# A gated cross-attention block: layer norm inside attention, hidden units on the partitions, int8 products

## The chip, the cores and the metric

The kernel runs on one core of a Trainium2 chip. The metric is the time of one execution on the device in microseconds (us). The engines are TensorE (PE; its weight loads are shown as PEld), VectorE (DVE), ScalarE (ACT), GpSimd (POOL) and SyncE (SP), which issues all DMAs here. Each engine works through its own list of instructions in order; semaphores tie the lists together.

## The reference

Four batches of 1024 tokens, width 512. A cross-attention with 8 heads of 64 over a context of 1024 keys is followed by a feed-forward part with ternary weights, 8-bit activations and a convolution over the tokens:

```python
x = x + tanh(g_x) * xattn(ctx, layernorm(x), mask, ...)      # 4 x 1024 x 512
x = x + tanh(g_f) * ffn(layernorm(x), w1, conv_w, conv_b, w2)

def act_quant(x):       # per token: the largest |x| becomes 127
    scale = 127.0 / clip(max(abs(x), axis=-1), 1e-05)
    return clip(round(x * scale), -128, 127) / scale
def bit_linear(x, w):  return einsum('bsd,hd->bsh', act_quant(x), weight_quant(w))

h = bit_linear(x, w1)                      # 512 -> 2048 hidden units
h = silu(depthwise_conv1d(h, conv_w, conv_b))   # 3 taps along the tokens, per unit
return bit_linear(h, w2)                   # 2048 -> 512
```

The second `act_quant` needs, for each token, the maximum over all 2048 hidden units before any of that token's values can be rounded.

## The kernel before

The program has three parts. First come the projections (up to about 670 us), which the change doesn't touch. Then comes attention, `c_pe`, `c_dve`, `c_act` and the POOL loop at L656 to L667 (to 1412 us), and last the feed-forward part, `ffn` on each engine.

**Attention.** A loop of 134 steps (`MACROS`, variable `s`), written out and the same on every engine, sets the order. 32 steps belong to one batch. A step has two units (`score`, `product`: 128 keys by 512 queries of a pair of heads) and two `tops`, which run 22 units ahead: they multiply keys and queries once more (L1244) into PSUM banks 4 and 5, and DVE takes the row minimum from them (L926) to give the softmax its shift. Each of the two banks holds one `tops`, so TensorE may write the next only when DVE has read the last (`dve_free4`, `dve_free5`). ACT takes the exponential of each unit (L684), POOL adds seven of each eight probability tiles to a sum (L667). Every fourth step the sums are turned into the scale of the result (L950 to L968). In the first eight steps of the next batch TensorE also does `project` (L1224 to L1226), eight token tiles of 128, whose result DVE adds to `bx` (`finish`, L975); SP stores `bx` to memory as x2.

**Feed-forward part.** Per batch: x2 comes back from memory as `xn`; DVE does the layer norm of the second half of the block there (`ln_steps`, L862 to L910), with 127/max per token; TensorE turns the rounded values (L1407). The steps for batch b+1 stand between those of batch b's last stage; those of batch 0 stand alone. Then come 16 tiles of 128 hidden units (the units on the partitions, 1024 tokens along the free axis): TensorE multiplies (`first`, L1419), DVE scales (`scaled`, L1158), ACT and POOL and DVE do the three taps (L800, L804, L672, L1179), TensorE turns the tile so that tokens lie on the partitions (L1448), ACT takes silu from PSUM (L823), DVE the maxima (L1163). When all 16 are through, the hidden values of 128 tokens at a time are rounded (L1168, L1170), shifted back to integers by ACT (L810, L815), turned again by TensorE (L1434), copied by ACT (L832, L840) and multiplied by w2 (L1461); DVE adds the result to x2 (L1207). The whole batch goes out in one DMA.

## Time and profile before

| | us |
|---|---|
| median of 3 runs (lowest to highest) | 1928.52 (1926.75 to 1930.60) |
| the profiled execution | 1929.86 |
| its span | 1928.0 |
| PE busy in the span | 1684.4 (87%) |
| DVE busy | 1216.9 (63%) |
| ACT busy | 780.3 (40%) |
| POOL busy | 729.0 (38%) |
| attention, last projected tile added | 1412.8 |
| first scaled tile of the feed-forward part | 1441.5 |

A part's busy share says which engine could bound it; the idle time ahead of an instruction, and the engine that ended it, say who waited for whom. The granted clock of TensorE has two levels here, 2.4 GHz (1.0 in the rows) and 1.2 GHz.

### The profile page before, as it was taken

To read this page: it belongs to the slowest core of one execution; us is meant where nothing else is said; L and a number is where in the kernel's file an instruction comes from. 1 tells how busy PE (TensorE), PEld (TensorE's weight loads), DVE (VectorE), ACT (ScalarE), POOL (GpSimd) and SP (SyncE) were. 2 spreads that over 40 slices of the span, in tenths; PEclk is the share of its full clock that TensorE was granted. 3 is DMA by queue.
4 is the path that set the end of the run, shared out by engine and by line. 5 is a ranking of instruction groups with operands and counts; after the bars stand their busy time and mean duration, and the time that the engine had idled before them with its cause. 6 is when DMAs were issued, how large, how long until landed. Compare 5 with 4: busy or idle time off the path is not lost.

```text
span 1928.0 us, 24398 instructions
## 1 busy us (share of the span) xinstructions
PE 1684.4 (87%) x8738; PEld 1038.8 (54%) x8738; DVE 1216.9 (63%) x2270; ACT 780.3 (40%) x793; POOL 729.0 (38%) x317
## 2 busy tenths in 40 slices
PE   6887899999997699999999999999856785967867
PEld 5666678888885344455445444544433443534434
DVE  6777645343433567755765676465269979799793
ACT  2111122222210044433442344245318766787676
POOL 1121000000000088866885688578606134062340
PEclk9989999999998599999999999999979798997988
DMA  6656547444444511114111412041130030120201
GB/s 233 229 181 206 179 170 243 154 149 152 171 145 152 180 56 56 56 66 143 56 57 66 143 57 100 12 143 35 44 131 1 1 131 0 38 92 0 88 1 44
DMA packets 104676, 200.59 MB, mean 104 GB/s; under 512 B 7568, under 2 KB 27024, under 8 KB 104592
## 3 DMA queue, kind: packets, MB, share of 16 engines
q1 hardware_dynamic: 104592, 199.49, 29.5%
q8 instruction: 50, 0.82, 0.2%
q14 instruction: 34, 0.28, 0.0%
HBM read 127.90 MB, written 71.57 MB: 103 GB/s over the span
## 4 chain that ended last, share of the span: by engine, by line
PE 62%; issue 19%; POOL 7%; DVE 6%; DMA 5%; SPq 1%; ACT 1%; POOLq 0%; DVEq 0%; ACTq 0%
PE ps L1260 13%; PE ps L1272 12%; PE ps L1224 9%; PE ps L1226 9%; PE ps L1225 9%; PE ps L1244 6%; DMA wraw<-in_w2T 5%; POOL h_first L672 4%; POOL h_third L672 2%; PE ps L1285 2%; DVE junk L926 1%; PE ps L1461 1%; DVE h_first L1179 1%; POOL acc L667 1%; DVE gp L1158 1%
## 5 line engine op out<-in xcount | busy, mean ns | idle before, releaser
L667 POOL TENSOR_TENSOR acc<-acc,pr 128x1024 f32<-128x1024 f32 x192 | 457.7, 2384 | 118.7 <-ACT pr L684 99.6
L684 ACT ACTIVATE pr<-ps,mcol 128x1024 f32<-128x1024 f32 x256 | 284.3, 1114 | 405.1 <-PE ps L1260 402.3
L926 DVE CUSTOM_DVE_ANT_0 junk<-ps,mbias 128x512 bf16<-128x512 f32 x512 | 333.4, 689 | 171.8 <-PE ps L1244 168.0
L1272 PE MATMUL ps<-pr,vv 128*64 128x512 f32 x1024 | 273.3, 616 | 0.0
L672 POOL TENSOR_TENSOR h_first<-h_first,last_tap 128x1024 f32<-128x1024 f32 x44 | 104.8, 2385 | 306.2 <-ACT last_tap L804 306.2
L650 POOL MEMSET nmt<- 128x128 f32 x1 | 0.2, 204 | 449.1 <-DMA w_ternary<-wtb 449.1
L1244 PE MATMUL ps<-kh,qh 64*128 64x512 f32 x512 | 136.8, 475 | 26.3 <-DVE nmv L926 17.6
L1244 PEld LDWEIGHTS ps<-kh,qh 64*128 64x128 f32 x512 | 57.5, 193 | 148.3 <-issue 101.7
L1419 PE MATMUL ps<-xiT,w1q 128*128 128x512 bf16 x512 | 125.1, 393 | 5.9 <-ACT xiT L790 5.9
L1461 PE MATMUL ps<-w2q,hq 128*128 128x512 bf16 x512 | 120.8, 390 | 2.5 <-ACT hq L840 1.8
L667 POOL TENSOR_TENSOR acc<-pr 128x1024 f32<-128x1024 f32 x32 | 76.8, 2399 | 110.8 <-ACT pr L684 110.8
L1260 PE MATMUL ps<-qh,kh 64*128 64x512 f32 x512 | 116.2, 445 | 0.0
L1448 PE MATMUL ps<-ident,h_first 128*128 128x128 f32 x352 | 57.8, 317 | 66.2 <-DVE h_first L1179 51.8
L1260 PE MATMUL ps<-qh,kl 64*128 64x512 f32 x512 | 102.5, 392 | 0.0
L1260 PE MATMUL ps<-maug,aug 64*128 64x512 f32 x512 | 102.3, 391 | 0.0
L1260 PE MATMUL ps<-ql,kh 64*128 64x512 f32 x512 | 102.0, 390 | 0.0
L1224 PE MATMUL ps<-chh,wsh 128*128 128x512 f32 x256 | 99.7, 389 | 1.7 <-DVE chl L1091 1.7
L1224 PE MATMUL ps<-wsh,chh 128*128 128x512 f32 x256 | 99.7, 389 | 0.3 <-DVE cst L1133 0.3
L1226 PE MATMUL ps<-wsh,chl 128*128 128x512 f32 x256 | 99.6, 389 | 0.0
L1225 PE MATMUL ps<-wsl,chh 128*128 128x512 f32 x256 | 99.6, 389 | 0.0
L1225 PE MATMUL ps<-chl,wsh 128*128 128x512 f32 x256 | 99.6, 389 | 0.0
L1226 PE MATMUL ps<-chh,wsl 128*128 128x512 f32 x256 | 99.6, 389 | 0.0
(152 smaller groups left out, 3179.7 us busy)
## 6 DMA issues: line engine op xcount, KB each, us to landing
craw<-in_ctxT SPq DMA_DIRECT2D x8, 2048.0 KB, 9.7
xa<-in_x SPq DMA_DIRECT2D x8, 1024.0 KB, 6.4
wraw<-in_w1T SPq DMA_DIRECT2D x16, 512.0 KB, 7.3
...
q_split<-kqh SPq DMA_DIRECT2D x32, 256.0 KB, 2.0
q_split<-kql SPq DMA_DIRECT2D x32, 256.0 KB, 2.3
...
k_split<-kqh SPq DMA_DIRECT2D x32, 256.0 KB, 2.2
```

The costliest lines, as they stand in the source:

```text
L667: nc.gpsimd.tensor_tensor(acc[:, blk % 2, :], first, pr[:, (8 * blk + j) % NP, :], ALU.add).then_inc(pool_acc, 1)
L672: nc.gpsimd.tensor_tensor(h[j % 3], h[j % 3], last_tap[j % 2][:], ALU.add).then_inc(pool_tap, 1)
L684: act.activation(pr[:, u % NP, :], ps[:, 2 * (u % 2):2 * (u % 2) + 2, :].rearrange("p a t -> p (a t)"), ACT.Exp, bias=mcol[:, (u // 64) * ...
L926: dve.tensor_tensor_reduce(out=junk[:, e, :], in0=ps[:, 4 + e, :], in1=mbias[:, b % 2, kk * CH:(kk + 1) * CH], scale=-1.0, scalar=3.0e38, ...
L1224: pe.matmul(acc, lh, rh, start=k == 0, stop=False)
L1225: pe.matmul(acc, lh, rl, start=False, stop=False)
L1226: last = pe.matmul(acc, ll, rh, start=False, stop=k == n - 1)
L1244: last = pe.matmul(ps[:, 4 + e, :], qh[g % 3][64 * e:64 * e + 64, i * P:(i + 1) * P], kh[g % 3][64 * e:64 * e + 64, kk * CH:(kk + 1) * CH] ...
L1260: last = pe.matmul(ps[:, 2 * (u % 2) + e, :], of_keys[64 * e:64 * e + 64, :], of_tokens[64 * e:64 * e + 64, :], start=w == 0, stop=w == 3)
L1272: last = pe.matmul(ps[64 * e:64 * e + 64, 6 + blk % 2, :], vv[:, g % 2, j, 64 * e:64 * e + 64], pr[:, u % NP, e * CH:(e + 1) * CH], start= ...
L1419: last = pe.matmul(ps[:, 2 * (j % 2) + t, :], w1q[:, k, j * P:(j + 1) * P], xiT[:, k, t * 512:(t + 1) * 512], start=k == 0, stop=k == KD - 1)
L1461: last = pe.matmul(ps[:, i % 2, :], hq[:, i % 2, j, :], w2q[:, j, :], start=j == 0, stop=j == KH - 1)
```

## The change

The layer norm of batches 0 to 2 moves into attention, in the steps of the following batch; it works in `bx` itself, so x2 isn't read back for it. The turned integers go to memory (`xt_d`) and come back as `xiT`, already turned. For the last batch the same work stands between the hidden tiles of batch 0.

Beside that the second half of the feed-forward part is built anew. The hidden values stay with the units on the partitions (`hh`). TensorE turns each tile once, in float32, only so that DVE can take the maxima over the units (`highest`). The scale of each token is then spread over all partitions by TensorE (`spread`, into banks 6 and 7); DVE multiplies each unit tile by it and writes int8 (`quantised`), ACT widens int8 to bfloat16 (`widen`), and the product takes the tile as it lies. Six token tiles are multiplied in the stage itself, the two that find no free PSUM banks are left for the opening of the next batch (`left_over`). The scaling happens in PSUM in place, the taps read PSUM, and the output goes out in 32 DMAs of 128 tokens.

```diff
+        STATS, NORMS, ROUNDS, XT = {}, {}, {}, {}
+        for b in range(B - 1):
+            m0 = 32 * (b + 1)
+            MOMENTS[m0 + NT], RSTD[m0 + NT + 2], SCALES[m0 + NT + 11] = b, b, b
+            for i in range(NT):
+                STATS[m0 + i] = b, i
+                NORMS[m0 + NT + 3 + i] = b, i
+                ROUNDS[m0 + NT + 12 + i] = b, i
+                XT[m0 + NT + 13 + i] = b, i
+        MP = [6, 0, 6, 0, 6, 0] + [(2, 6, 0)[j % 3] for j in range(KH - 6)]
+        EARLIER = {j: max(i for i in range(j) if MP[i] == MP[j]) for j in range(KH) if MP[j] in MP[:j]}
+        PLACE = [0, 1, 2, 3, 4, 5, 2, 3]
...
@@ SP, in attention
                 if g % PAIRS == 1 and b:
                     store_x2(b - 1)
-                    sp.wait_ge(sp_x2_out, 16 * b)
-                    sp.dma_start(bx[:], base_d[b * S:(b + 1) * S, :].rearrange("(j p) d -> p j d", p=P)).then_inc(sp_bx, 16)
+                if g % PAIRS == 3 and b:
+                    store_xt(b - 1)
+                    load_bx(b)
                 if g + 1 < NG:
                     max_rows(g + 1)
...
@@ ACT, in attention
             for s in range(MACROS):
+                if s - 1 in XT:
+                    turned(*XT[s - 1])
                 for a in range(2):
                     if 2 * s + a < UNITS:
                         exp(2 * s + a)
                     if a == 0 and s - 2 in ZBLK:
                         upper(ZBLK[s - 2])
+                if s - 1 in MOMENTS:
+                    deviation(act, MOMENTS[s - 1])
+                if s in ROUNDS:
+                    integers(act, *ROUNDS[s])
...
@@ DVE, at the end of a step of attention
+                if s in NORMS:
+                    normalise(dve, *NORMS[s])
+                    tallest(dve, *NORMS[s])
+                if s in ROUNDS:
+                    rounded(dve, *ROUNDS[s])
...
+        def normalise(dve, b, i):
+            dve.wait_ge(dve_rs, b + 1)
+            dve.wait_ge(sp_x2_out, 16 * (b + 1))
+            dve.tensor_scalar(bx[:, i, :], bx[:, i, :], mv2[:, i, 0:1], rs2[:, 1, i:i + 1], ALU.subtract, ALU.mult).then_inc(dve_nm, 1)
+        def rounded(dve, b, i):
+            dve.wait_ge(dve_sc, 4 * (b + 1))
+            dve.tensor_scalar(bx[:, i, :], bx[:, i, :], asc[:, i:i + 1], MAGIC, ALU.mult, ALU.add).then_inc(dve_xr, 1)
+        def integers(act, b, i):
+            act.wait_ge(dve_xr, NT * b + i + 1)
+            act.activation(bxi[:, i, 0:D], bx[:, i, :], ACT.Copy, bias=-MAGIC).then_inc(act_xi, 1)
+            def turned(b, i):
+                act.wait_ge(pe_xt, NT * b + i + 1)
+                act.activation(bxi[:, i, D:2 * D], ps[:, 5, :].bitcast(BF16)[:, 0:D], ACT.Copy).then_inc(act_xt, 1)
...
@@ TensorE, in attention: ahead of the first tops of a step, and at a step's end
+                if n >= LEAD and (n - LEAD) % 2 == 0 and (n - LEAD) // 2 - 1 in XT:
+                    b, i = XT[(n - LEAD) // 2 - 1]
+                    pe.wait_ge(act_xt, NT * b + i + 1)
...
+                if s in XT:
+                    b, i = XT[s]
+                    pe.wait_ge(dve_free5, use5["b", min(2 * s + LEAD, UNITS - 2) + 1] + 1)
+                    if b or i:
+                        pe.wait_ge(act_xt, NT * b + i)
+                    turn_xi(pe, b, i, 5, 0)
...
@@ TensorE, feed-forward part
+                unit_tile(b, 1)
+                for j in range(KH):
+                    if b and j < 4:
+                        left_over(b - 1, 6 + j // 2, j % 2)
+                    if j + 2 < KH:
+                        unit_tile(b, j + 2)
+                    if j >= 2:
+                        turn_h(b, j - 2)
+                turn_h(b, KH - 2)
+                turn_h(b, KH - 1)
+                pe.wait_ge(dve_hm, 5 * b + 4)
+                spread(hsc, 6).then_inc(pe_inv, 1)
+                if b + 1 < B:
+                    spread(adq[:, b + 1, :], 0).then_inc(pe_row, 1)
...
+                for j in range(KH):
+                    pe.wait_ge(act_hq, KH * b + j + 1)
+                    if j == KH - 1 and b + 1 < B:
+                        unit_tile(b + 1, 0)
+                    product(b, j, range(6))
...
@@ DVE, feed-forward part
+                scaled(b, 0)
+                if b:
+                    for i in range(4):
+                        finish(b - 1, i)
+                scaled(b, 1)
+                if b:
+                    finish(b - 1, 4)
+                    finish(b - 1, 5)
+                for j in range(KH):
+                    if b and j in (2, 4):
+                        finish(b - 1, 5 + j // 2)
+                    first_tap(b, j)
+                    if j == KH - 1:
+                        third_tap(b, j)
                     if j >= 3:
+                        highest(b, j - 3)
+                    if j + 2 < KH:
+                        scaled(b, j + 2)
...
+                for j in range(KH - 3, KH):
+                    highest(b, j)
+                unit_scales(b)
+                for j in range(KH):
+                    quantised(b, j)
```

How the lists move, at three places. First ACT in attention, in the part of a batch where the norm is rounded and turned. Before (L684 is the exponential, L692 the copy of a scaled result):

```order
L692 ACTIVATE uh<-un 128x512
L684 ACTIVATE pr<-ps,mcol 128x1024 x8
L692 ACTIVATE uh<-un 128x512
L684 ACTIVATE pr<-ps,mcol 128x1024 x8
L692 ACTIVATE uh<-un 128x512
```

Now (L703 is the exponential; L694 is `integers`, L715 `turned`, L711 the copy of a scaled result):

```order
L703 ACTIVATE pr<-ps,mcol 128x1024 x2
L694 ACTIVATE bx<-bx 128x512
L715 ACTIVATE bx<-ps 128x512
L703 ACTIVATE pr<-ps,mcol 128x1024 x2
L694 ACTIVATE bx<-bx 128x512
L715 ACTIVATE bx<-ps 128x512
L703 ACTIVATE pr<-ps,mcol 128x1024
L711 ACTIVATE uh<-un 128x512
```

Between the two exponentials of one step and the two of the next there are now the copy that follows DVE's rounding and, behind it, the copy out of bank 5.

Second, DVE in attention, one step in which a block's sums are finished. Before (L926 is the row minimum and its readout, L954 to L963 the scale):

```order
L926 ISA nmv 128x1
L954 RECIPROCAL zr<-zt 128x16
L956 STREAM_TRANSPOSE rb<-zr 128x512
L926 ISA junk,nmv<-ps,mbias 128x512
L926 ISA nmv 128x1
L926 ISA junk,nmv<-ps,mbias 128x512
L926 ISA nmv 128x1
L963 TENSOR_TENSOR un<-ps,rb 128x512
L926 ISA junk,nmv<-ps,mbias 128x512
```

Now (L878 is `normalise`, L882 `tallest`, L908 the row minimum, L945 the former L963):

```order
L936 RECIPROCAL zr<-zt 128x16
L938 STREAM_TRANSPOSE rb<-zr 128x512
L908 ISA junk,nmv<-ps,mbias 128x512
L908 ISA nmv 128x1
L908 ISA junk,nmv<-ps,mbias 128x512
L908 ISA nmv 128x1
L945 TENSOR_TENSOR un<-ps,rb 128x512
L878 TENSOR_SCALAR bx<-bx,mv_118,rs_119 128x512
L882 TENSOR_REDUCE amax<-bx 128x1
L908 ISA junk,nmv<-ps,mbias 128x512
```

Two instructions stand between the last row minimum of one step and the first of the next; in the later steps of the batch it is one, L895 (`rounded`).

Third, DVE at the end of a batch's 16 tiles in the feed-forward part. Before:

```order
L1179 SCALAR_TENSOR_TENSOR h_first<-gp,convw,h_first 128x1024
L1163 TENSOR_REDUCE hmax<-hT 128x8 x3
L1186 TENSOR_REDUCE hm<-hmax 128x8
L1188 TENSOR_SCALAR hm<-hm 128x8
L1190 RECIPROCAL hsc<-hm 128x8
L1192 TENSOR_SCALAR hsc<-hsc 128x8
L1193 TENSOR_SCALAR hdq<-hm,cst 128x8
L1168 TENSOR_SCALAR hT<-hT,hsc 128x1024 x2
L1170 TENSOR_SCALAR hT<-hT,hsc 128x2048 x3
```

Now (L1149 is `scaled`, L1153 `first_tap`, L1163 `highest`, L1182 `quantised`, L1190 `finish`):

```order
L1153 SCALAR_TENSOR_TENSOR hh<-ps,convw,hh 128x1023
L1158 SCALAR_TENSOR_TENSOR hh<-ps,convw,hh 128x1023
L1163 TENSOR_REDUCE hmax<-ps 128x8 x4
L1167 TENSOR_REDUCE hm<-hmax 128x8
L1169 TENSOR_SCALAR hm<-hm 128x8
L1171 RECIPROCAL hsc<-hm 128x8
L1173 TENSOR_SCALAR hsc<-hsc 128x8
L1174 TENSOR_SCALAR hdq<-hm,cst 128x8
L1182 TENSOR_TENSOR q_126<-hh,ps 128x1024 x16
L1149 TENSOR_TENSOR ps<-ps,row 128x1024
L1190 SCALAR_TENSOR_TENSOR x2t<-ps,hdq,x2t 128x512 x4
L1149 TENSOR_TENSOR ps<-ps,row 128x1024
```

The maxima at the end each follow a turned tile in the one pair of banks 4 and 5, and the finished outputs of the batch stand among the first tiles of the next. In the new code `unit_tile(b, j)` waits for `first_tap` of tile `EARLIER[j]`, the last to hold its banks, and `turn_h(b, j)` for `highest(b, j - 1)`.

## Rows read from the trace of the kernel before

**Rows 1.** Busy time in stretches: span, then PE, PEld, DVE, ACT, POOL; clock, DMA

```profile
750.00:1340.00 590.00, 585.58 (x3287) 284.93 (x3285) 370.85 (x1004) 240.72 (x234) 427.94 (x181) 1.00 0.22 79
1563.00:1637.00 74.00, 48.44 (x248) 28.57 (x246) 68.36 (x50) 53.71 (x49) 38.69 (x16) 0.88 0.20 72
```

**Rows 2.** Timeline of one step of attention: start, duration, engine, line, [idle before]

```profile
916.48 0.49 PE L1244 MATMUL ps<-kh,qh 64*128 64x512 f32 x2
917.15 2.38 POOL L667 TENSOR_TENSOR acc<-pr 128x1024 f32<-128x1024 f32 x1 [1.34 <-ACT pr L684]
918.24 0.08 DVE L926 DVE_READ_ACCUMULATOR2_ANT nmv<- 128x1 f32 x1
918.95 0.39 PE L1244 MATMUL ps<-kh,qh 64*128 64x512 f32 x2
919.49 0.69 DVE L926 CUSTOM_DVE_ANT_0 junk<-ps,mbias 128x512 bf16<-128x512 f32 x1 [0.89 <-PE ps L1244]
```

**Rows 3.** Timeline: POOL adds and DVE instructions that overlap them

```profile
771.71 2.39 POOL L667 TENSOR_TENSOR acc<-pr 128x1024 f32<-128x1024 f32 x1 [1.33 <-ACT pr L684]
773.07 1.58 DVE L937 TENSOR_SCALAR mbias<-mbias 128x1024 f32<-128x1024 f32 x1
...
811.89 2.39 POOL L667 TENSOR_TENSOR acc<-pr 128x1024 f32<-128x1024 f32 x1 [1.34 <-ACT pr L684]
831.96 2.39 POOL L667 TENSOR_TENSOR acc<-pr 128x1024 f32<-128x1024 f32 x1 [1.31 <-ACT pr L684]
...
1606.49 2.36 POOL L672 TENSOR_TENSOR h_first<-h_first,last_tap 128x1024 f32<-128x1024 f32 x1 [2.20 <-ACT last_tap L804]
1607.56 2.38 DVE L1179 SCALAR_TENSOR_TENSOR h_first<-gp,convw,h_first 128x1024 f32<-128x1024 f32 x1
```

**Rows 4.** Groups of instructions after 1400 us: count, busy us, mean ns

```profile
L886 DVE TENSOR_SCALAR xn<-xn,mv,rs 128x512 f32<-128x512 f32 x32 | 15.0, 544 | 0.1
L891 DVE TENSOR_REDUCE amax<-xn 128x1 f32<-128x512 f32 x32 | 19.6, 683 | 0.0
L908 DVE TENSOR_SCALAR xn<-xn,asc 128x512 f32<-128x512 f32 x32 | 15.4, 480 | 0.0
L810 ACT ACTIVATE hi<-hT 128x1024 bf16<-128x1024 f32 x8 | 8.0, 1049 | 13.1 <-DVE hT L1168 13.1
```

**Rows 5.** Timeline between attention and the feed-forward part, and its third batch's start

```profile
1412.08 0.75 DVE L975 SCALAR_TENSOR_TENSOR bx<-ps,cst,bx 128x512 f32<-128x512 f32 x1 [3.17 <-PE ps L1226]
1441.49 1.23 DVE L1158 TENSOR_TENSOR gp<-ps,row 128x1024 f32<-128x1024 f32 x1 [5.32 <-PE ps L1419]
...
1684.71 1.23 DVE L1158 TENSOR_TENSOR gp<-ps,row 128x1024 f32<-128x1024 f32 x1 [3.63 <-PE ps L1419]
```

**Rows 6.** Timeline of a hidden tile in the second batch, and DVE two tiles on

```profile
1602.88 1.21 DVE L1158 TENSOR_TENSOR gp<-ps,row 128x1024 f32<-128x1024 f32 x1
1604.01 1.36 DVE L1179 SCALAR_TENSOR_TENSOR h_third<-gp,convw,h_third 128x1024 f32<-128x1024 f32 x1
1604.12 1.24 ACT L800 ACTIVATE h_first<-gp,convb,convw 128x1024 f32<-128x1024 f32 x1
1605.50 1.09 PE L1448 MATMUL ps<-ident,h_third 128*128 128x128 f32 x8 [0.73 <-DVE h_third L1179]
...
1610.98 1.21 DVE L1158 TENSOR_TENSOR gp<-ps,row 128x1024 f32<-128x1024 f32 x1
```

**Rows 7.** Timeline: eight turns at the lower clock, and sixteen products at the higher

```profile
1632.13 1.97 PE L1448 MATMUL ps<-ident,h_first 128*128 128x128 f32 x8 [0.35 <-DVE h_first L1179]
...
1676.68 3.62 PE L1461 MATMUL ps<-w2q,hq 128*128 128x512 bf16 x16
```

**Rows 8.** DMA issues: count, KB each, median us from issue to landing

```profile
v_full<-vst SPq DMA_DIRECT2D x32, 256.0 KB, 2.0
bx<-base SPq DMA_DIRECT2D x4, 2048.0 KB, 8.7
row_max<-mt SPq DMA_DIRECT2D x16, 16.0 KB, 1.4
```

More of the change, by code:

```diff
@@ L21 @@
 BF16 = mybir.dt.bfloat16
+INT8 = mybir.dt.int8
 ALU = mybir.AluOpType
@@ L269, in flamingo_gated_block @@
         dve_free5 = sem("dve_free5")
[L270 removed]
+        dve_top = sem("dve_top")
         dve_inv = sem("dve_inv")
@@ new lines, in taps @@
+            def taps(b, j):
+                act.wait_ge(dve_g, KH * b + j + 1)
+                act.activation(hh[:, j, :], flat(MP[j]), ACT.Identity, bias=convb[:, j:j + 1], scale=convw[:, j, 1:2]).then_inc(act_tap, 1)
+                if j == KH - 1:
+                    return
+                n = (KH - 1) * b + j
+                if n >= 2:
+                    act.wait_ge(pool_tap, n - 1 if j >= 2 else (KH - 1) * b)
+                act.activation(tap[:, j % 2, 0:S - 1], flat(MP[j])[:, 1:S], ACT.Copy, scale=convw[:, j, 2:3]).then_inc(act_tap, 1)
@@ new lines, in _ @@
+            scale_row(0)
+            for b in range(B):
+                for j in range(KH):
+                    taps(b, j)
+                    if j >= 2:
+                        silu(b, j - 2)
+                    if b == 0 and j == 1:
+                        deviation(act, LAST_B)
+                    if b == 0 and j >= NT:
+                        integers(act, LAST_B, j - NT)
+                silu(b, KH - 2)
+                silu(b, KH - 1)
+                if b + 1 < B:
+                    scale_row(b + 1)
+                if b == 0:
+                    for u in range(NT // 2):
+                        turned_last(u)
+                for j in range(KH):
+                    widen(b, j)
@@ L1210, in _, with scaled @@
-            for step in ln_steps(dve, 0):
-                step()
-            for s in range(3):
-                dve.memset(gp[:, s, 0:1], 0.0)
-                dve.memset(gp[:, s, S + 1:S + 2], 0.0)
-            with dve.Fori(0, B - 1) as b:
-                ffn(b, True)
-            ffn(B - 1, False)
+            def scaled(b, j):
+                dve.wait_ge(pe_h, KH * b + j + 1)
+                if j == 0:
+                    dve.wait_ge(act_row, b + 1)
+                dve.tensor_tensor(flat(MP[j]), flat(MP[j]), row[:, b % 2, :], ALU.mult).then_inc(dve_g, 1)
@@ L1220, in split_mm @@
+            for i in range(NT):
+                finish(LAST_B, i)
         def split_mm(pe, acc, lhs, rhs, n):
@@ L1227, in split_mm, with turn_xi @@
             return last
-        def ln_row(pe, b):
-            pe.wait_ge(dve_ln, b * LN_DVE_N + LN_DVE["diag"])
-            for t in range(2):
-                last = pe.matmul(ps[:, 2 + t, :], ones[:], diag[:, 4 * t:4 * t + 4, :], start=True, stop=True)
-            last.then_inc(pe_row, 1)
+        def turn_xi(pe, b, i, bank, part):
+            pe.wait_ge(act_xi, NT * b + i + 1)
+            for k in range(KD):
+                last = pe.transpose(ps[:, bank, :].bitcast(BF16)[:, (part * KD + k) * P:(part * KD + k + 1) * P], bxi[:, i, k * P:(k + 1) * P], identb[:])
+            last.then_inc(pe_xt, 1)
         def c_pe(pe):
@@ L1470, in _, with spread @@
-            ln_row(pe, 0)
-            for u in range(NT // 2):
-                ln_turn(0, u)
-            pe.wait_ge(sp_ffw, 32)
-            with pe.Fori(0, B - 1) as b:
-                ffn(b, True)
-            ffn(B - 1, False)
+            def spread(cols, bank):
+                for i in range(NT):
+                    last = pe.matmul(ps[:, bank + i // 4, i % 4 * P:(i % 4 + 1) * P], cols[:, i:i + 1].broadcast_to([P, P]), ident[:],
+                                     start=True, stop=True)
+                return last
@@ L1479 @@
+            for i in (6, 7):
+                for part in range(2):
+                    left_over(LAST_B, i, part)
 _INS = ["x", "ctxT", "mask", "mask_cols", "g_x", "g_f", "wsT", "bk_cols", "b_v", "wtT", "bq_cols", "woT", "b_out",
```

564 lines of the change are left out of this document (247 added, 317 removed).

## The prediction

> **What bounds the kernel now.** I read the busy time in stretches first. From 750 to 1340 us TensorE is busy 585.6 of 590 us at the full clock, DVE 370.9, POOL 427.9 [rows 1]. So attention is bound by TensorE, and whatever makes TensorE wait there lengthens the kernel. In the hidden tiles of the feed-forward part DVE is busy 68.4 of 74 us and TensorE 48.4 [rows 1]; DVE sets the pace there. Then I read timelines. Two first scalings two batches apart, 1441.49 and 1684.71, give 121.6 us a batch [rows 5]. Between the last `finish` of attention (1412.08 + 0.75) and the first scaling lie 28.7 us in which the layer norm of batch 0 runs alone [rows 5]. Two things can be won, then: that gap, and part of the 486.5 us from 1441.5 to the end of the span. The price falls in attention.
>
> **Part 1, the gap.** After the change TensorE spreads the scales at once (8 small matmuls, estimate 1.6 us), ACT copies the row (1024 columns, like the 1.05 us of [rows 4]), and DVE scales: first scaling 3.5 us after `finish`, not 28.7. That is -25.2 us.
>
> **Part 2, the hidden tiles.** Before, two tiles take 8.10 us (1602.88 to 1610.98), 4.05 each [rows 6]. DVE's instructions follow each other closer than their lengths: 1.13 us after a 1.21 (1602.88 to 1604.01) [rows 6]. Now DVE does `scaled`, `first_tap` and `highest`, 1.13 + 1.20 + 1.13 = 3.46 us. The second length is that of the unblocked tap, 1.36 at most [rows 6]; the longer one of 2.38 overlaps a POOL add [rows 3], and the new tap reads PSUM. That in-place writing to PSUM costs no more than writing to SBUF no row shows; I take the 1.21 and give 4.05 a tile as the upper end. TensorE needs 8 x 0.22 for the matmuls (16 in 3.62 [rows 7]) and 1.09 for the turns [rows 6], 2.9 us: hidden. ACT has two taps and a silu, each below the 1.24 of [rows 6], some 3.3 us: just hidden.
>
> Not all tiles run at 3.46. Tiles 0 to 5 use two pairs of banks, so DVE waits in a circle: tap 1.2, matmuls of tile j+2 2.1 (1.75 plus the drain), scaling 1.2: 4.5 us. In a batch after the first:
> opening, two scalings, six outputs of 0.67 (0.75 long [rows 5]) and one wait for the banks, 7.0; five tiles at 4.5, 22.5; nine at 3.46, 31.1; last two taps, third tap and two maxima, 6.0; three turns that alternate with their maxima in one pair of banks, 3 x 2.4, and 2.2 more since TensorE drops to the lower clock when it idles there (eight turns 1.97 against 1.09 [rows 6, 7]), 9.4; the scale arithmetic 1.3; `spread` 2.9 at the lower clock (estimate, 8 loads and matmuls). Sum 80.2.
> Then `quantised` makes a tile in 1.13, ACT widens it in 1.05 [rows 4], TensorE multiplies six token tiles in 6 x 0.22 = 1.3 us. TensorE bounds this stage, and it starts late: the second `spread`, the row copy and the first widening come first, 4.8; 15 products, two of them at half clock, 22; the next batch's first tile, 2. In all 109.0 us, against 121.6.
> Batch 0 has no outputs of an earlier batch among its tiles but the last batch's norm: 8 x (0.54 + 0.68 + 0.48) [rows 4] and some waits for POOL, net 18, and four more copies of ACT ahead of the first widening, 4: 131. The last batch ends with 32 products left over (6.9), the outputs and one DMA of 256 KB (2.0 [rows 8]): 118. Sum 131 + 109 + 109 + 118 = 467 against 486.5: -19.5 us. Bounds: -35 if the clock stays up in the last turns and first products, 0 if the nine tiles stay at 4.05.
>
> **Part 3, the norm in attention.** TensorE begins a `tops` at 916.48, DVE has read both banks at 918.32, the next begins at 918.95, and DVE starts on it at 919.49 after 0.89 idle [rows 2]. Work put into that gap costs TensorE what exceeds about 0.9 + 0.6 = 1.5 us; the 0.6 is 918.95 less 918.32, the time by which a bank is free too early. `normalise` and `tallest` are 0.54 + 0.68 = 1.22 [rows 4]: nothing, if nobody is in their way. But POOL is. A DVE `tensor_scalar` that began at 773.07 ended at 774.65, 0.55 after the POOL add that ran to 774.10, and took 1.58; the tap at 1607.56 ended 1.09 after POOL's 1608.85 [rows 3]. Both did their work after POOL's instruction, not beside it. POOL's seven adds of 2.39 fill 16.7 of the 20.07 us of four steps (811.89 to 831.96 [rows 3]), 83%. So `normalise` waits up to 2.39, on average half of it: 1.2 + 0.3 + 0.68 = 2.2, 0.7 over the gap, 24 times: +17 us (bounds 0 and 24 x 1.9 = 45).
>
> The Trainium skill ("SBUF — State Buffer", section "SBUF: two separate sides") says the port pair that DVE and GpSimd share is an exclusive lock for a whole instruction, against DVE instructions in a 2-port mode or with two SBUF inputs. The rows above agree, and the rule speaks against this change: both moved `tensor_scalar` are of that kind, while `quantised`, `scaled` and `highest` are not. Were it a sharing of bandwidth instead, a `normalise` would grow by tenths of a us, stay in the gap, and the sum would be that of the first rival.
>
> The rounding is dearer, since three engines hang on it. In the steps of XT, counted from the second `tops`: DVE free at 1.84; `rounded` waits for POOL, done at 3.6 (1.4 + 0.3); ACT, whose list has `integers` ahead of `turned` ahead of the next exponential, does `integers` by 4.3 and `turned`, out of bank 5, by 5.0 (512 columns, 0.6 each, from 1.05 for 1024 [rows 4]). TensorE may not start the next `tops` before that; it would be there at 2.47 [rows 2] + 0.27 for four turns. It stands 2.4 us, 2.7 with the turns. Seven steps in each of batches 0 and 1; batch 2's fall where no `tops` are left (they run 22 units ahead of 256) and cost 0.3, as do the last steps. 14 x 2.7 + 10 x 0.3 = +41 us. Bounds: 14 x 1.3 + 3 = 21 if POOL is never in the way, 14 x 4.1 + 3 = 60 if always by a whole add.
>
> DMAs: SP now loads `bx` (2 MB, 8.7 us [rows 8]) only some 2.3 steps before the next group's scores, with `row_max` (1.4 [rows 8]) and its way back queued behind: 8.7 + 1.4 + 2.5 against 11.5 us, about 1.3 late, twice: +3. `x2` is stored in time for `normalise`. The statistics stand in the steps of `project`, where DVE idles 3 us before each `finish` [rows 5]: 0. The small scale arithmetic: +1. Attention: 17 + 41 + 3 + 1 = +62.
>
> **Sum.** 1929.9 (the profiled execution, span 1928.0 and 1.9 around it; 1.3 above the median) - 25.2 - 19.5 + 62 = 1947; as a median 1946.
>
> **Rivals.**
> Faster: the adds of POOL don't meet the moved instructions. As steps stretch, POOL idles more, and it already has 1.34 us idle ahead of a block's first add [rows 2]. Then `normalise` costs 0 and the XT steps 21, attention +22: 1928.5 - 44.7 + 22 = 1906. It decides at an attention cost of 45 us; below that the change wins. Against it: 83% of POOL's time is taken, and ACT's order alone gives the 21.
> Slower still: the hidden tiles gain nothing (writing into PSUM dear, or ACT's 3.3 us late): 9 x 0.59 x 4 = 21 more, 1967.
> The clock: with turns and matmuls at the lower clock a tile needs 1.97 + 3.5 = 5.5 us of TensorE, 2.0 more than 3.46, 64 times: +130, 2076. Against it: TensorE kept the higher clock at 2.9 of 4.05 us [rows 6], and 2.9 of 3.46 is more.
>
> **How the numbers follow.** The forecast 0.55 (own range 1924 to 1972), the first rival 0.33, the second 0.08, the clock 0.04. Slower by over 0.2% (the 3.9 us that a measurement can tell from no change): most of the forecast, 0.46, the last two, 0.12, a little of the first rival, 0.03: 0.61. Within: 0.06 + 0.02 = 0.08. Faster: 0.03 + 0.28 = 0.31. The range takes most of the first rival and the second: 1899 to 1977.
>
> **What would show it.** Right: ACT's `turned` ends about 5 us after the second `tops` of its step, and TensorE idles 2 to 3 us before the next; `normalise` and `rounded` in attention last on average well over 1 us; first scaling within 4 us of the last `finish`; a batch of the feed-forward part takes about 109 us with tiles of 4.5 and then 3.46. Wrong: these two at 0.5 us each in attention, attention longer by under 45 us, or a batch period away from 100 to 118.

## The result and the profile after

The changed kernel takes 1973.2 us (median of four runs, 1971.9 to 1978.0) where the kernel before took 1929.6 on the same chip: ratio 1.0233, interval 1.0212 to 1.0254. I had forecast 1946 with a range of 1899 to 1977. The direction and the range held; the loss is 43.6 us where I had 17.

The two profiled executions differ by 42.9 us of span (1970.9 less 1928.0). Four landmarks divide them: POOL's first addition of attention, the last `finish` (L957), the first scaling of the feed-forward part (L1149) and the end. Here are the rows of after, from the timelines of POOL and DVE (start, duration, engine, line, idle before and what ended it):

```profile
673.74 2.39 POOL L680 TENSOR_TENSOR acc<-pr 128x1024 f32<-128x1024 f32 x1 [55.57 <-ACT pr L703]
...
1485.14 0.75 DVE L957 SCALAR_TENSOR_TENSOR bx<-ps,cst,bx 128x512 f32<-128x512 f32 x1 [2.42 <-PE ps L1243]
1489.83 1.23 DVE L1149 TENSOR_TENSOR ps<-ps,row 128x1024 f32<-128x1024 f32 x1 [3.20 <-PE ps L1450]
...
1616.61 1.23 DVE L1149 TENSOR_TENSOR ps<-ps,row 128x1024 f32<-128x1024 f32 x1 [10.76 <-PE ps L1450]
1730.32 1.23 DVE L1149 TENSOR_TENSOR ps<-ps,row 128x1024 f32<-128x1024 f32 x1 [9.49 <-PE ps L1450]
1842.59 1.23 DVE L1149 TENSOR_TENSOR ps<-ps,row 128x1024 f32<-128x1024 f32 x1 [7.07 <-PE ps L1450]
```

| stage | before | after | difference | forecast |
|---|---|---|---|---|
| attention, POOL's first addition to last `finish` | 737.9 | 811.4 | +73.5 | +62 |
| last `finish` to first scaling | 29.4 | 4.7 | -24.7 | -25.2 |
| feed-forward part, first scaling to end | 486.5 | 481.1 | -5.4 | -19.5 |

(The rest, -0.5, lies before attention.) The gap is as forecast. Attention costs 11.5 more, the feed-forward part gives 14 less.

In attention TensorE is no longer the engine that is always busy. The busy time of the stretch of [rows 1], now:

```profile
750.00:1340.00 590.00, 554.45 (x2985) 264.42 (x2981) 398.67 (x1003) 236.09 (x245) 376.25 (x160) 0.98 0.22 76
```

TensorE stands still for 35.6 us of it, before for 4.4. What it waits for shows in the waits of that attention (engine, line, what it waited for: us in total, times, longest). ACT's copy that makes integers (L694) waits for DVE's rounding (L895), and TensorE's product for the row minima (L1263) for ACT's copy of the turned tile (L715):

```profile
ACT bx L694 <- DVE bx L895: 78.6, 21, 5.2
PE ps L1263 <- ACT bx L715: 21.5, 13, 2.5
```

Two such steps that follow each other in the timeline of after; POOL is in the way in the first and not in the second:

```profile
969.74 4.87 POOL L680 TENSOR_TENSOR acc<-acc,pr 128x1024 f32<-128x1024 f32 x2 [4.19 <-ACT pr L703]
972.85 2.05 DVE L895 TENSOR_SCALAR bx<-bx,asc 128x512 f32<-128x512 f32 x1
976.09 0.50 PE L1263 MATMUL ps<-kh,qh 64*128 64x512 f32 x2 [2.45 <-ACT bx L715]
...
982.93 0.40 PE L1249 MATMUL ps<-identb,bx 128*128 128x128 bf16 x4
...
983.68 0.45 DVE L895 TENSOR_SCALAR bx<-bx,asc 128x512 f32<-128x512 f32 x1
984.16 0.63 ACT L694 ACTIVATE bx<-bx 128x512 bf16<-128x512 f32 x1 [5.21 <-DVE bx L895]
984.70 0.58 ACT L715 ACTIVATE bx<-ps 128x512 bf16<-128x512 bf16 x1
985.33 0.50 PE L1263 MATMUL ps<-kh,qh 64*128 64x512 f32 x2 [0.87 <-ACT bx L715]
...
986.36 4.88 POOL L680 TENSOR_TENSOR acc<-acc,pr 128x1024 f32<-128x1024 f32 x2 [4.38 <-ACT pr L703]
```

In the first, POOL's two additions run to 974.6, the rounding takes 2.05 us where it takes 0.45 in the second, and TensorE stands still for 2.45 us where it does for 0.87. The second shows what ACT's order does by itself. TensorE has turned the tile by 983.3. Its copy (L715) needs nothing else, but ACT's list has L694 ahead of it, and that waits for a rounding of another tile; the copy, the exponential and the next product for the minima come that much later: 984.70 for the copy instead of 983.3. ACT had idled 5.2 us before.

How much each kind of step costs is read from POOL's first addition in every block of four steps. In after:

```profile
916.67 2.35 POOL L680 TENSOR_TENSOR acc<-pr 128x1024 f32<-128x1024 f32 x1 [1.34 <-ACT pr L703]
...
963.19 2.37 POOL L680 TENSOR_TENSOR acc<-pr 128x1024 f32<-128x1024 f32 x1 [1.42 <-ACT pr L703]
...
1026.95 2.36 POOL L680 TENSOR_TENSOR acc<-pr 128x1024 f32<-128x1024 f32 x1 [4.49 <-ACT pr L703]
1048.98 2.39 POOL L680 TENSOR_TENSOR acc<-pr 128x1024 f32<-128x1024 f32 x1 [1.33 <-ACT pr L703]
```

The same blocks in `no_norm` below, which has no layer norm in attention and whose attention is within 1.5 us of before's:

```profile
915.17 2.39 POOL L680 TENSOR_TENSOR acc<-pr 128x1024 f32<-128x1024 f32 x1 [1.33 <-ACT pr L703]
...
955.06 2.39 POOL L680 TENSOR_TENSOR acc<-pr 128x1024 f32<-128x1024 f32 x1 [1.35 <-ACT pr L703]
...
995.25 2.39 POOL L680 TENSOR_TENSOR acc<-pr 128x1024 f32<-128x1024 f32 x1 [1.33 <-ACT pr L703]
1015.37 2.39 POOL L680 TENSOR_TENSOR acc<-pr 128x1024 f32<-128x1024 f32 x1 [1.35 <-ACT pr L703]
```

A block stands between the shown ones in the first two distances. The two blocks with a `normalise` (steps 11 to 18 of the batch) take 46.52 against 39.89, +6.6 for eight steps. The two with the turnings take 63.76 against 40.19, +23.6, and the next, which holds the last copy, 22.03 against 20.12, +1.9. Over all three batches, against before: normalise +19.8, turnings of batches 0 and 1 +48.4, the last blocks (batch 2's rounding and turning) +5.3; sum 73.5.

In the blocks with a `normalise` an instruction that the change didn't touch grew too: L950 (`lower`), once a block, whose two inputs and output are in SBUF. The same one in after and in no_norm (where its line is L952):

```profile
940.82 2.29 DVE L950 TENSOR_TENSOR ul<-un,uh 128x512 fp32r<-128x512 f32 x1
```

```profile
934.16 0.69 DVE L952 TENSOR_TENSOR ul<-un,uh 128x512 fp32r<-128x512 f32 x1
```

POOL's addition runs from 940.21 to 942.56 in after; in no_norm the next one starts only at 935.22. Three times in this batch, in these two blocks and right behind them, L950 now falls beside an addition (917.47, 940.82, 963.37: 2.10, 2.29, 2.73 us); in no_norm and small_pool the same three take 0.69. DVE is busy 42.4 of the 46.5 us of the two blocks (its waits for POOL counted in), in no_norm 27.4 of 39.9.

In the feed-forward part the hidden tiles run at exactly the forecast pace. DVE in the third batch, where [rows 6] had 8.10 for two tiles:

```profile
1764.51 1.22 DVE L1149 TENSOR_TENSOR ps<-ps,row 128x1024 f32<-128x1024 f32 x1
...
1767.96 1.22 DVE L1149 TENSOR_TENSOR ps<-ps,row 128x1024 f32<-128x1024 f32 x1
```

3.45 us a tile. The loss is elsewhere: at the openings, where the outputs of the batch before (L1190) are finished, and at the end, where those of the last batch are. DVE after 1616.61, and the PE work behind it:

```profile
1617.75 2.72 DVE L1190 SCALAR_TENSOR_TENSOR x2t<-ps,hdq,x2t 128x512 f32<-128x512 f32 x4
...
1623.62 0.75 DVE L1190 SCALAR_TENSOR_TENSOR x2t<-ps,hdq,x2t 128x512 f32<-128x512 f32 x1 [1.24 <-DMA x2t<-x]
1625.72 0.75 DVE L1190 SCALAR_TENSOR_TENSOR x2t<-ps,hdq,x2t 128x512 f32<-128x512 f32 x1 [1.35 <-DMA x2t<-x]
1626.38 1.27 DVE L1153 SCALAR_TENSOR_TENSOR hh<-ps,convw,hh 128x1023 f32<-128x1023 f32 x1
...
1627.71 3.60 PE L1450 MATMUL ps<-xiT,w1q 128*128 128x512 bf16 x8 [4.88 <-DVE hh L1153]
```

The first tap starts 9.8 us after the scaling, and 11.0 in the two later openings, forecast 7.0. x2 has four tiles in SBUF; the load of tile k+3 waits until the store of tile k-1 is through, and with loads and stores in turn each takes 3.5 us to land (after's DMA table: `x2t<-x` and `out<-x2t`, 256 KB each), where I had taken 2.0 from [rows 8]. TensorE, idle for 4.9 us, restarts at the lower clock: 3.60 for eight matmuls that take 1.90 at 1619.20. At the end the last four outputs start 2.2 to 2.6 us apart (1960.28, 1962.83, 1965.08, 1967.55), each behind its load. In all DVE waits for these loads 20.6 us in 13 waits.

### The profile page after: what moved, and what is told of

Read it like the earlier page. It is cut to its first block and busy times, and to the rows that moved or that the text cites. A ratio compares the mean times of both kernels' runs of the same rounds, so it can differ in the third digit from the quotient of the medians.

```text
span 1970.9 us, 22933 instructions
## 1 busy us (share of the span) xinstructions
PE 1701.0 (86%) x8338; PEld 1028.1 (52%) x8338; DVE 1233.3 (63%) x2260; ACT 732.1 (37%) x825; POOL 715.3 (36%) x313
## 5 line engine op out<-in xcount | busy, mean ns | idle before, releaser
L908 DVE CUSTOM_DVE_ANT_0 junk<-ps,mbias 128x512 bf16<-128x512 f32 x512 | 332.3, 686 | 154.5 <-PE ps L1263 151.5
L703 ACT ACTIVATE pr<-ps,mcol 128x1024 f32<-128x1024 f32 x256 | 283.8, 1115 | 361.6 <-PE ps L1279 352.9
L1291 PE MATMUL ps<-pr,vv 128*64 128x512 f32 x1024 | 280.0, 630 | 0.0
L686 POOL TENSOR_TENSOR hh<-hh,tap 128x1023 f32<-128x1023 f32 x60 | 141.5, 2358 | 316.6 <-DVE hh L1153 259.2
L1263 PE MATMUL ps<-kh,qh 64*128 64x512 f32 x512 | 152.6, 489 | 57.0 <-DVE nmv L908 24.8
L1263 PEld LDWEIGHTS ps<-kh,qh 64*128 64x128 f32 x512 | 63.3, 194 | 199.6 <-issue 88.3
L1461 PE MATMUL ps<-ident,hh 128*128 128x128 f32 x512 | 81.5, 311 | 65.9 <-DVE hmax L1163 65.9
L1450 PE MATMUL ps<-xiT,w1q 128*128 128x512 bf16 x384 | 100.3, 409 | 29.3 <-DVE hh L1153 24.4
L1149 DVE TENSOR_TENSOR ps<-ps,row 128x1024 f32<-128x1024 f32 x64 | 78.4, 1225 | 67.9 <-PE ps L1450 67.9
L820 ACT ACTIVATE hh<-ps,convb,convw 128x1024 f32<-128x1024 f32 x64 | 77.1, 1205 | 102.8 <-DVE ps L1149 102.8
L1461 PEld LDWEIGHTS ps<-ident,hh 128*128 128x128 f32 x512 | 66.5, 161 | 91.7 <-issue 69.6
```

Source lines behind the costliest of these rows:

```text
L686: nc.gpsimd.tensor_tensor(hh[:, j, 0:S - 1], hh[:, j, 0:S - 1], tap[:, j % 2, 0:S - 1], ALU.add).then_inc(pool_tap, 1)
L703: act.activation(pr[:, u % NP, :], ps[:, 2 * (u % 2):2 * (u % 2) + 2, :].rearrange("p a t -> p (a t)"), ACT.Exp, bias=mcol[:, (u // 64) * ...
L908: dve.tensor_tensor_reduce(out=junk[:, e, :], in0=ps[:, 4 + e, :], in1=mbias[:, b % 2, kk * CH:(kk + 1) * CH], scale=-1.0, scalar=3.0e38, ...
L1149: dve.tensor_tensor(flat(MP[j]), flat(MP[j]), row[:, b % 2, :], ALU.mult).then_inc(dve_g, 1)
L1263: last = pe.matmul(ps[:, 4 + e, :], qh[g % 3][64 * e:64 * e + 64, i * P:(i + 1) * P], kh[g % 3][64 * e:64 * e + 64, kk * CH:(kk + 1) * CH] ...
L1291: last = pe.matmul(ps[64 * e:64 * e + 64, 6 + blk % 2, :], vv[:, g % 2, j, 64 * e:64 * e + 64], pr[:, u % NP, e * CH:(e + 1) * CH], start= ...
```

## The experiments

Ratios are to the kernel before on the same chip; "against after" is the difference of the two ratios (after 1.0233) times 1929.6. The kernels ran on four chips, so it is the ratios that are compared. The block columns are what the blocks of normalise steps and of turnings (batches 0 and 1) take more than before, in one profiled execution each. That of act_order took 1931.0 us, 7.7 less than its median: 42.0 less than after's, 33.6 of it in attention.

| kernel | us | ratio, interval | against after | normalise | turnings |
|---|---|---|---|---|---|
| after | 1973.2 | 1.0233, 1.0212 to 1.0254 | | +19.8 | +48.4 |
| no_norm | 1894.1 | 0.9840, 0.9815 to 0.9864 | -75.8 | -0.1 | 0.0 |
| act_order | 1938.7 | 1.0074, 1.0056 to 1.0091 | -30.7 | +19.9 | +17.4 |
| small_pool | 1922.1 | 0.9983, 0.9971 to 0.9995 | -48.2 | +1.6 | +23.7 |
| order_pool | 1905.3 | 0.9891, 0.9855 to 0.9927 | -66.0 | +1.5 | +8.1 |
| order_split | 1955.6 | 1.0144, 1.0089 to 1.0200 | -17.2 | +31.3 | +26.5 |
| on_act | 1908.9 | 0.9888, 0.9840 to 0.9936 | -66.6 | +3.5 | +8.6 |
| x2_eight | 1954.5 | 1.0151, 1.0131 to 1.0172 | -15.8 | +19.8 | +48.4 |
| on_act_x2 | 1896.0 | 0.9823, 0.9778 to 0.9868 | -79.1 | +3.3 | +8.7 |
| on_act_x2_again | 1896.0 | 0.9820, 0.9804 to 0.9836 | -79.7 | +3.2 | +8.8 |
| best | 1917.0 | 0.9947, 0.9934 to 0.9960 | -55.2 | +3.4 | +28.3 |

**no_norm: attention without the layer norm.** The loop is the one that fills STATS, NORMS, ROUNDS and XT; what sets the semaphores of the missing work is not shown.

```
-        for b in range(B - 1):
+        for b in range(0):
-                    sp.wait_ge(act_xt, NT * b + i + 1)
+                    sp.wait_ge(sp_x2_out, 16 * (b + 1))
-                                 bxi[:, i, D:2 * D].rearrange("p (k t) -> p k t", k=KD)).then_inc(sp_xt_out, 16)
+                                 w1q[:, :, i * P:(i + 1) * P]).then_inc(sp_xt_out, 16)
```

> Leaves out the whole layer norm of batches 0 to 2 inside attention (statistics, normalise, maxima, rounding, integers, turning, and the copies of the turned tiles); what it stores as the turned tiles is other data of the same size, at the end of the batch's output, and the feed-forward part runs as in the changed kernel (the turned integers of the last batch are made in the tail as before, with the others' scales set to 1). All of the lengthening of attention is the layer norm's: the last finish of attention falls from 1485.1 to 1412 or 1415 us, the time to about 1900. A rival: the DMA queue's new loads and stores cost a part that stays, 5 to 10 us, and the time is 1905 to 1910.

-75.8 us. Attention takes 739.3 us from POOL's first addition to the last `finish`, 1.5 more than before, with the loads and stores of the change still there (the turned tiles' store sends other data of the same size). So the layer norm is practically all of attention's lengthening, and the moved DMAs are at most 1.5 of it; the rival of 5 to 10 falls.

**act_order: the copy of the turned tile no longer behind the rounding.**

```
                     if a == 0 and s - 2 in ZBLK:
                         upper(ZBLK[s - 2])
+                    if a == 0 and s - 1 in ROUNDS:
+                        integers(act, *ROUNDS[s - 1])
...
-                if s in ROUNDS:
-                    integers(act, *ROUNDS[s])
```

> Same computation as the changed kernel. Only ScalarE's order differs in the attention of batches 1 and 2: the copy that makes the integers of a tile (L694) stands behind the first exponential of the next step instead of at the step's end, so the copy of the turned tile (L715), which the row maxima's next product waits for, no longer stands behind VectorE's rounding. Theory A (the order on ScalarE makes the round trip long: rounding, integers, turned copy, product of the maxima): the sixteen steps with a turning fall from 2.9 us extra each to about 1, the time falls by about 28 us, to 1945. Rival B (the rounding is late because GpSimd's addition holds VectorE off, and everything behind it is late whatever ScalarE's order is): less than 6 us, 1967 to 1973. What the profile is to show under A: ScalarE's wait for bx of VectorE (82.5 us in 22 waits) falls below 30 us.

-30.7, theory A. The turnings fall from +48.4 to +17.4, 1.1 us a step, the normalise blocks don't move. ACT's wait for the rounding is 3.0 us in two waits between 954 and 1020 us, 30.0 in seven in after; over the whole of attention it is 3.9, in after 78.6. The instructions are the same; only ACT's list differs. From the timeline of this kernel:

```profile
993.38 0.40 PE L1249 MATMUL ps<-identb,bx 128*128 128x128 bf16 x4
...
993.71 2.56 DVE L895 TENSOR_SCALAR bx<-bx,asc 128x512 f32<-128x512 f32 x1
993.82 0.60 ACT L715 ACTIVATE bx<-ps 128x512 bf16<-128x512 bf16 x1 [1.29 <-PE ps L1249]
...
994.75 0.40 PE L1263 MATMUL ps<-kh,qh 64*128 64x512 f32 x2
...
996.30 0.63 ACT L694 ACTIVATE bx<-bx 128x512 bf16<-128x512 f32 x1 [0.23 <-DVE bx L895]
```

Here a rounding of 2.56 us, held back by POOL (two additions, 991.09 to 995.99), runs beside the copy and TensorE's next product: TensorE doesn't see it.

**small_pool: POOL's additions cut to a sixteenth of their columns.** One takes 0.32 us instead of 2.38.

```
-  nc.gpsimd.tensor_tensor(acc[:, blk % 2, :], first, pr[:, (8 * blk + j) % NP, :], ALU.add)
+  nc.gpsimd.tensor_tensor(acc[:, blk % 2, 0:64], first[:, 0:64], pr[:, (8 * blk + j) % NP, 0:64], ALU.add)
```

> GpSimd adds only the first 64 of 1024 columns of each exponential (the rest of the softmax's sums is left out), so its additions hold VectorE off for a tenth of the time. Attention is otherwise the changed kernel's. Theory A (the layer norm's instructions cost mainly by the order of work and by their own length in VectorE's row, GpSimd's hold adds a part): the steps with a normalise fall from 0.83 to near 0.2 us extra, those with a rounding from 2.9 to about 2, in all -30 to -40 us, about 1938. Rival B (GpSimd's hold on VectorE is nearly all of it): -60 us or more, 1910. Rival C (the hold costs nothing beside TensorE): within 5 us of 1973.

-48.2, between A and B, and A's share for each kind of step was too small. The normalise steps lose all but 1.6 of 19.8 us; the turnings halve. The groups of DVE's instructions on `bx` between 900 and 1450 us (count, busy us, mean ns, idle before), first in act_order:

```profile
L895 DVE TENSOR_SCALAR bx<-bx,asc 128x512 f32<-128x512 f32 x24 | 33.2, 1388 | 0.0
L878 DVE TENSOR_SCALAR bx<-bx,mv,rs 128x512 f32<-128x512 f32 x24 | 25.2, 1052 | 0.0
...
L882 DVE TENSOR_REDUCE amax<-bx 128x1 f32<-128x512 f32 x24 | 16.5, 686 | 0.8
```

and in small_pool (its lines are one higher):

```profile
L883 DVE TENSOR_REDUCE amax<-bx 128x1 f32<-128x512 f32 x24 | 16.5, 686 | 0.8
L879 DVE TENSOR_SCALAR bx<-bx,mv,rs 128x512 f32<-128x512 f32 x24 | 12.8, 531 | 0.0
L896 DVE TENSOR_SCALAR bx<-bx,asc 128x512 f32<-128x512 f32 x24 | 11.2, 470 | 0.0
```

The `tensor_scalar` falls from 1052 to 531 and from 1388 to 470 ns; even one of eight columns (`amax`, three times), from 1269 to 161. The reduction on the same tile is the same to the ns. The Trainium skill ("SBUF — State Buffer", section "SBUF: two separate sides", under "Who interferes with whom") says just this: `tensor_scalar` can take the port pair that DVE shares with GpSimd, a `tensor_reduce` on trn2 never does. The rows agree.

**order_pool: both together.** act_order's and small_pool's edits.

> act_order with GpSimd adding only 64 of 1024 columns (the rest of the softmax's sums is left out). The question is whether the two causes, ScalarE's order and GpSimd's hold on VectorE, are together all of the turning steps' price. Additive theory: act_order left 0.8 to 1.8 us per turning step, small_pool left 1.4; together 0 to 0.3 each, attention is within 4 us of that of the kernel without a layer norm (no_norm, 1894.1), 1895 to 1900. Rival (a third cause: the product for the row maxima that waits for the turned tile's copy): 0.6 us or more per turning step stays, 1905 or more.

1905.3: the additive theory fails, attention is 10.2 us longer than no_norm's and not 4. The rival's time is met by a little, its cause isn't: the turnings keep 8.1 us, 0.5 a step, but between 954 and 1020 us no product waits for the turned tile's copy. ACT's order took 31.0 of the 48.4, POOL's hold 24.7, both 40.3 and not 55.7: they overlap. My reading, argued from the lists, is that a rounding that POOL holds back costs most where the copy stands behind it. With act_order POOL's hold is still worth 9.3 (17.4 less 8.1). What stays is mostly the turning's own time on TensorE. Two steps' first score products in order_pool, with the turning (L1250) between them, then the same two in no_norm:

```profile
972.72 0.51 PE L1280 MATMUL ps<-qh,kh 64*128 64x512 f32 x2
...
977.45 0.40 PE L1250 MATMUL ps<-identb,bx 128*128 128x128 bf16 x4
977.77 0.50 PE L1280 MATMUL ps<-qh,kh 64*128 64x512 f32 x2
```

```profile
971.51 0.50 PE L1284 MATMUL ps<-qh,kh 64*128 64x512 f32 x2
...
976.22 0.50 PE L1284 MATMUL ps<-qh,kh 64*128 64x512 f32 x2
```

The step takes 5.05 us with the turning and 4.71 without, and TensorE doesn't stand still ahead of L1250. Sixteen times 0.34 are 5.4 of the 8.1 us. In the waits between 954 and 1020 us the turning's weight load stands against DVE's minimum for 4.1 us, but that load overlaps other products and its wait costs nothing here.

**order_split: normalise in the middle of the step.** Besides act_order's edit:

```
                     if n < UNITS:
                         tops(n)
+                    if a == 0 and s in NORMS:
+                        normalise(dve, *NORMS[s])
...
-                    normalise(dve, *NORMS[s])
                     tallest(dve, *NORMS[s])
```

> Same computation as the changed kernel. ScalarE's order as in act_order (1938.7 us), and on VectorE the normalise stands behind the step's first pair of row maxima, its maximum still at the step's end, so that each single instruction falls into a gap of VectorE's row. Theory A (what the 24 normalise steps cost, 0.83 us each, is two instructions in one gap of VectorE's row that is too short for both): they fall to 0.3, -13 us, 1926. Rival B (each of the two instructions waits for GpSimd's addition to end, wherever it stands: in small_pool the same steps cost 0.1): no gain, 1936 to 1941, or a loss.

Against theory A, and rival B's "or a loss": 13.5 us slower than act_order. I had argued with the room that a gap leaves; what counts is when POOL begins. DVE and POOL of this kernel:

```profile
927.11 2.38 DVE L878 TENSOR_SCALAR bx<-bx,mv,rs 128x512 f32<-128x512 f32 x1
```

```profile
926.84 4.86 POOL L680 TENSOR_TENSOR acc<-acc,pr 128x1024 f32<-128x1024 f32 x2 [1.46 <-ACT pr L703]
```

In its new place `normalise` comes 0.3 us after the addition that the same step's exponential has released, and waits out nearly all of it; its mean goes from 1052 to 1464 ns. The turnings rose as well, from 17.4 to 26.5 us, and no run says by what.

**on_act: the two `tensor_scalar` on ACT.** Besides act_order's edit, for batches 0 to 2 (the semaphores, DVE's small product for `nb2` and the lines taken from DVE's list are not shown):

```
+        def normed(act, b, i):
+            act.activation(bx[:, i, :], bx[:, i, :], ACT.Identity, bias=nb2[:, i:i + 1], scale=rs2[:, 1, i:i + 1])
+        def whole(act, b, i):
+            act.activation(bx[:, i, :], bx[:, i, :], ACT.Copy, bias=MAGIC, scale=asc[:, i:i + 1])
...
+                    if a == 0 and s in NORMS:
+                        normed(act, *NORMS[s])
                     if a == 0 and s - 1 in ROUNDS:
                         integers(act, *ROUNDS[s - 1])
+                    if a == 0 and s in ROUNDS:
+                        whole(act, *ROUNDS[s])
```

> Same computation as the changed kernel. ScalarE's order as in act_order, and the normalise and the rounding of batches 0 to 2 are done by ScalarE (scale and bias from a small product on VectorE) instead of VectorE, each behind the first exponential of its step, so that only the maximum of each tile is left on VectorE, beside GpSimd's additions. ScalarE's row then holds 2.2 us of exponentials and 1.9 of the layer norm in a step of 5. Theory (VectorE's instructions on two tiles in SBUF pay for GpSimd's additions, ScalarE's don't): the normalise steps fall from 0.83 to between 0 and 0.4, the turning steps to below 0.5, in all -20 to -30 us from act_order's 1938.7, 1912. Rival (ScalarE's longer row delays the exponentials, which the scores' banks wait for): less than 8 us, 1931 or more.

1908.9, the theory; the turning steps keep 0.54 us each, just above its 0.5. With POOL at full work the price is nearly that of order_pool (12.1 against 9.6 us in the two columns). On ACT they take 800 and 712 ns:

```profile
L696 ACT ACTIVATE bx<-bx,nb,rs 128x512 f32<-128x512 f32 x24 | 19.2, 800 | 0.0
L700 ACT ACTIVATE bx<-bx,asc 128x512 f32<-128x512 f32 x24 | 17.1, 712 | 0.8 <-DVE asc L905 0.8
```

longer than DVE alone needs, shorter than DVE beside POOL.

**x2_eight: eight tiles for x2.** The turned integers of the third batch are also loaded ahead of the first x2 tiles now (not shown).

```
-        x2 = sb("x2t", [P, 4, D], F32)
+        x2 = sb("x2t", [P, NT, D], F32)         # in the place of bx, loaded once bx has been turned
...
-                if k >= 1 and k + 3 < NT * B:
-                    sp.wait_ge(sp_out[(k - 1) % 4], 16 * ((k - 1) // 4 + 1))
-                    load_x2(k + 3)
+                if k >= 1 and k + NT - 1 < NT * B:
+                    sp.wait_ge(sp_out[(k - 1) % NT], 16 * ((k - 1) // NT + 1))
+                    load_x2(k + NT - 1)
```

> Same computation as the changed kernel. The feed-forward part has eight tiles for x2 instead of four (in the place of the sums' tile, loaded once the last batch has been turned), so a finish no longer waits for a load that stands behind a store that has only just begun. Theory A (the term missing from the prediction: the finishes wait for the loads, 20.6 us in 13 waits, and TensorE restarts at the lower clock behind them): batches 1 and 2 fall from 113.0 to about 109, the last from 128.3 to about 119, in all -14 to -20 us, about 1956. Rival B (the finishes would wait for products and banks instead, since the openings are bound by the two bank pairs that the finishes leave free): no more than 4 us, 1969 to 1973.

-15.8, theory A. DVE's opening of the second batch in this kernel (lines one higher), to be laid beside that of after:

```profile
1616.42 1.23 DVE L1150 TENSOR_TENSOR ps<-ps,row 128x1024 f32<-128x1024 f32 x1 [9.24 <-PE ps L1451]
1617.56 2.72 DVE L1191 SCALAR_TENSOR_TENSOR x2t<-ps,hdq,x2t 128x512 f32<-128x512 f32 x4
...
1622.10 1.40 DVE L1191 SCALAR_TENSOR_TENSOR x2t<-ps,hdq,x2t 128x512 f32<-128x512 f32 x2
1623.41 1.27 DVE L1154 SCALAR_TENSOR_TENSOR hh<-ps,convw,hh 128x1023 f32<-128x1023 f32 x1
```

The opening takes 6.99 us. The batches take 127.0, 109.0, 109.1 and 119.3 (first scalings at 1489.44, 1616.42, 1725.42 and 1834.55, the span ends at 1953.8) against 126.8, 113.7, 112.3 and 128.3 in after: over half of the gain is in the last one. Loads and stores still take 3.6 and 3.3 us to land, so the gain is in the number of tiles and not in faster transfers.

**on_act_x2 and on_act_x2_again: the two gains together.**

> Same computation as the changed kernel: on_act with the eight x2 tiles of x2_eight. The two gains lie in different stages and add: on_act's time less 15.8 us (measured between the changed kernel and x2_eight), 1896 if on_act gives 1912, so 1.7% below the kernel before.

> The kernel of on_act_x2 once more, in five rounds, since its ratio came with an interval of 0.9 per cent: if the two gains add as the block times say, the ratio to the kernel before is 0.983 to 0.984; a ratio above 0.986 would say that a part of what the first runs showed was the other chip's.

They add: 1896.0 both times, and the five-round ratio of 0.982 (0.9804 to 0.9836) puts it 1.8% below the kernel before. It computes what the kernel before computes. The change pays once DVE's waits for POOL, ACT's for the rounding and DVE's for x2 are out of the way.

**best: the turning one place later.** On top of on_act_x2:

```
                     if 2 * s + a < UNITS:
                         score(2 * s + a)
+                    if a == 0 and s - 1 in XT:
+                        ...
+                        turn_xi(pe, b, i, 5, 0)
-                    if a == 0 and 2 * s + LEAD < UNITS:
+                    if a == (s - 1 in XT) and 2 * s + LEAD < UNITS:
                         tops(2 * s + LEAD)
```

> Same computation as the changed kernel: on_act_x2 (1896.0 us) with one more change of order. The turning of the integers (TensorE) stands behind the first scores product of the next step instead of ahead of it, its copy on ScalarE behind the step's first exponential, and the product for the row maxima behind the second scores product of that step. In on_act the turning waits on TensorE for VectorE's maximum on the same bank, with all scores queued behind it, and each turning step keeps 0.5 to 0.8 us over one without. Theory (that wait is the rest of the price): 16 steps by 0.5, -8 us, 1888. Rival (the copy of the turned tile now comes later, so the row maxima's product waits for it instead, and the rest stays): 1893 to 1898, or a loss.

Against the theory, and the rival's "or a loss": about 24 us slower than on_act_x2 by the ratios, 21 by the medians. As in order_pool, TensorE had not stood still ahead of the turning in on_act_x2, so there was little to win. Its weight load no longer waits, but the product for the minima comes behind the second scores; between 954 and 1020 us DVE now waits for it 25.1 us in 14 waits (on_act_x2: 16.6 in 19) and the blocks with turnings take 26.2 and 25.9 us instead of 23.6 and 21.1.

```profile
DVE junk L923 <- PE ps L1278: 25.1, 14, 3.0
```

DVE's minimum, TensorE's next product and the bank between them form a circle; I take it that the later product lengthens it, which no further run tests.

## Why the prediction was wrong in size

**Part 1 held:** -24.7 for -25.2; the first scaling starts 3.9 us after the last `finish` has ended.

**Part 2, the step that failed is the opening, and with it the end of the last batch.** "Six outputs of 0.67 ... and one wait for the banks, 7.0", and for the last batch "one DMA of 256 KB (2.0)", treated x2 as always there. The changed code has four tiles for it (`x2t`), and I counted SP's transfers for `bx` but not these. The term was put at nothing and is 15.8 us by x2_eight. With it gone, the feed-forward part takes 464.4 where the sum said 467: 109.0 and 109.1 for the two batches of 109.0, 127.0 for 131, 119.3 for 118, and within them the opening 6.99 for 7.0, the tiles 3.45 for 3.46 and, among the first ones, 4.4 to 5.1 for 4.5.

**Part 3, `normalise`:** +19.8 for +17, and the nearness is luck. That POOL is what makes these steps dear is shown by small_pool (1.6 stay) and on_act (3.5). But the wait for POOL, "on average half of it: 1.2", was 0.52: the mean is 1052 ns in after and act_order, against 531 with POOL's additions cut. With 0.69 for `tallest` and the forecast's gap of 1.5 the 24 lengths give 0.3 us a step, and it was 0.83. The gap is that of one step without the sums of a block; the sum left out the other instructions of DVE's list, of which L950 lost 1.4 to 2.0 us three times a batch. How much of the 0.83 each makes no run separates. Nor was the wait a mean over phases: DVE and POOL are both set going by what TensorE and ACT finish, and order_split, with `normalise` at another place in the step, paid 31.3 for the same instructions.

**Part 3, the turnings, mis-sized:** +53.7 (48.4 and 5.3 in the last blocks) for +41. The signs named came: TensorE idled 2.45 us in the step shown, and the rounding took 1220 ns on average. A turning step costs 3.0 and not 2.7, and all sixteen of batches 0 and 1 count, since a batch's last copy also stands before the next step's product; the last batch's eight cost 0.7 and not 0.3. The bound "21 if POOL is never in the way" was 23.7 plus the last blocks' 2.0 in small_pool. ACT's order, of which the prediction had made a part of the chain, is the larger cause of these steps' price, 31.0 alone against 24.7 for POOL's; over all of attention POOL's is the larger, since the normalise steps are its own.

**DMAs and small arithmetic:** +4 forecast, at most 1.5 in no_norm, and in after the blocks counted above already make up the whole 73.5. (The forecast's 8.7 + 1.4 + 2.5 less 11.5 is 1.1 and not 1.3.) Together: 2.8 more for the normalise, 12.7 for the turnings, 4 less here, so 11.5 in attention; 14.1 in the feed-forward part; 0.5 in the gap; less 0.5 ahead of attention. That is the 26 us between the forecast for a profiled execution, 1947, and the 1973.0 of this one.

**The rivals.** The first (POOL not in the way: attention +22) is what small_pool makes of it, +26.6; it didn't come true by itself. Its argument did in part: between 750 and 1340 us POOL's busy share fell from 73% to 64% as the steps stretched. Tiles that stay at 4.05 and a clock that falls among them are excluded by the 3.45. The lower clock was met where it was expected, at the last turns (1.94 for eight at 1569.84, 1573.19 and 1576.53), and also at the openings.
